# An attention-like recommendation layer on one core: spreading row weights half a pair nearer to their row sums

## What is computed

```python
outer = jnp.einsum('bi,bnj->bnij', candidate_ad, goods).reshape(Bs, Ns, Ks * Ks)
k_b = jnp.broadcast_to(candidate_ad[:, None, :], (Bs, Ns, Ks))
h1 = jnp.concatenate((k_b, goods, outer), axis=-1)
act = jax.nn.sigmoid(h1 @ W1 + b1)          # 36 hidden values
weight = act @ W2 + b2                       # one weight per good
out = jnp.sum(goods * weight, axis=1)        # (2048, 32)
```

## Time and profile before

| | us |
|---|---|
| median of 3 runs | 270.11 |
| lowest and highest | 269.48, 270.95 |
| the profiled execution, device time | 268.84 |
| its span, first to last instruction | 267.0 |
| PE busy | 254.5 (95%) |
| ACT busy | 236.6 (89%) |
| POOL busy | 196.6 (74%) |
| DVE busy | 193.8 (73%) |

### The profile page before, as it was taken

The page is one execution under the profiler, slowest core; times in us unless marked ns, Lnnn a source line. Parts: engine busy times, 40 slices in busy tenths (PEclk is TensorE's granted clock), DMA queues, the critical chain, the costliest instruction groups (busy, mean ns, idle before and its releaser), DMA issues.

```text
span 267.0 us, 18217 instructions
## 1 busy us (share of the span) xinstructions
PE 254.5 (95%) x7492; PEld 150.3 (56%) x7492; DVE 193.8 (73%) x1108; ACT 236.6 (89%) x658; POOL 196.6 (74%) x349
## 2 busy tenths in 40 slices
PE   7998999999999999999999999999999999999971
PEld 2425666565565665656656666556565565665630
DVE  0890277777777877877777778777787777877886
ACT  2897999999999999999999999999999999999840
POOL 1300787887887888788788788878878878887872
PEclk9999999999999999999999999999999999999996
DMA  5880766787777777777777777777777877777200
GB/s 204 253 300 16 230 196 199 242 229 210 241 224 211 237 220 227 230 218 230 211 223 237 211 236 226 212 239 217 219 224 221 234 219 225 225 210 231 65 0 11
DMA packets 38195, 54.84 MB, mean 205 GB/s; under 512 B 4240, under 2 KB 37904, under 8 KB 38032
## 3 DMA queue, kind: packets, MB, share of 16 engines
q1 hardware_dynamic: 37872, 54.15, 67.1%
q10 hardware_dynamic: 288, 0.32, 0.3%
HBM read 54.19 MB, written 0.26 MB: 204 GB/s over the span
## 4 chain that ended last, share of the span: by engine, by line
PE 91%; ACT 2%; DMA 2%; DVE 2%; issue 1%; POOL 1%; POOLq 0%; DVEq 0%
PE z_ps L337 28%; PE w_ps L384 26%; PE x_ps L360 16%; PE s_ps L422 6%; PE x_ps L422 6%; PE z_ps L289 2%; ACT act L495 2%; DMA act<-w_outer 2%; PE s_ps L337 2%; DVE goods L535 2%; PE s_ps L289 1%; PE x_ps L289 1%; PE x_ps L302 1%; PE w_ps L289 0%; POOL top L255 0%
## 5 line engine op out<-in xcount | busy, mean ns | idle before, releaser
L495 ACT ACTIVATE act<-z_ps,bias 128x200 f32<-128x200 f32 x448 | 149.8, 441 | 13.0 <-PE z_ps L337 7.6
L535 DVE CUSTOM_DVE_ANT_0 goods<-s_ps,goods 128x200 f32<-128x200 f32 x248 | 80.5, 362 | 30.9 <-PE w_ps L422 30.9
L337 PE MATMUL z_ps<-goods,wm_ring 32*32 32x200 f32 x3360 | 77.8, 339 | 1.7 <-issue 1.6
L255 POOL TENSOR_SCALAR top<-whole,consts 128x200 bf16<-128x200 f32 x64 | 50.1, 782 | 22.4 <-DVE whole L527 16.3
L337 PEld LDWEIGHTS z_ps<-goods,wm_ring 32*32 32x32 f32 x3360 | 46.1, 103 | 20.6 <-issue 11.9
L535 DVE CUSTOM_DVE_ANT_0 goods<-x_ps,goods 128x200 f32<-128x200 f32 x124 | 40.5, 364 | 22.7 <-PE s_ps L422 22.7
L384 PE MATMUL w_ps<-act,consts 128*32 128x200 f32 x1008 | 55.7, 339 | 0.0
L360 PE MATMUL x_ps<-goods,wx 128*32 128x200 f32 x1024 | 55.3, 333 | 0.0
L259 POOL TENSOR_SCALAR mid<-rest,consts 128x200 bf16<-128x200 f32 x64 | 50.1, 782 | 6.3
L535 DVE DVE_READ_ACCUMULATOR2_ANT out_stage<- 128x1 f32 x512 | 42.6, 83 | 0.0
L482 ACT ACTIVATE wm_ring<-wm 128x256 f32<-128x256 f32 x60 | 42.4, 706 | 0.0
(11 more groups left out here) (53 smaller groups left out, 212.7 us busy)
## 6 DMA issues: line engine op xcount, KB each, us to landing
goods<-goods_t SPq DMA_DIRECT2D x256, 200.0 KB, 2.7
act<-cand_r SPq DMA_DIRECT2D x1, 1024.0 KB, 5.4
act<-cand_u SPq DMA_DIRECT2D x1, 256.0 KB, 2.8
out_t<-out_stage SPq DMA_DIRECT2D x4, 64.0 KB, 2.6
consts<-small ACTq DMA_DIRECT2D x1, 164.5 KB, 5.4
act<-w_outer ACTq DMA_DIRECT2D x1, 144.0 KB, 5.6
pick_sb<-pick SPq DMA_DIRECT2D x1, 128.0 KB, 2.8
```

The source lines that it names most:

```text
L255: nc.gpsimd.tensor_scalar(top[:, :], whole[:, q % 2, :], m1, None, ALU.mult).then_inc(part_step, 1)
L337: last = nc.tensor.matmul(z_bank(slot, r)[32 * c:32 * c + 32, N * s:N * s + N], weights(slot, 32 * r, 4 * s + c), goods[32 * r:32 * r + 32 ...
L495: last = nc.scalar.activation(act[:, p % A_SLOTS, r, N * s:N * s + N], z_bank(p, r)[:, N * s:N * s + N], ACT.Sigmoid, bias=bias[:, r, p, s ...
L535: last = nc.vector.tensor_tensor_reduce(goods[:, q % G_SLOTS, v, :], s_bank(q, f, s)[:, N * i:N * i + N], goods[:, q % G_SLOTS, v, :], 1.0 ...
```

## The change

LAG stays 3, but the two places of an iteration take other halves. Place 0 of iteration p now spreads half f = 1 of pair p - 3, and place 1 half f = 0 of pair p - 2. DVE pools in the same new order. A pair's two halves are thus spread in place 1 of iteration q + 2 and place 0 of q + 3, instead of places 0 and 1 of q + 3. With it:

- Place 1 in the loop waits for stack_made and w_kept, place 0 for actx_done and pooled[1][0]. There is a place 1 in iteration 2 already.
- Behind the loop: spread(64, 0), row_sums(64), spread(64, 1), both places of 65, and place 0 of 66.
- For pair 63, DVE makes top and rest itself, into tiles of their own (top_last, rest_last), right behind keep(63); POOL makes mid and stack.
- The banks of a place stay as they were in the loop; the semaphores pooled are now counted by place, and SP's waits follow.

```diff
-        def s_bank(q, f, s):
-            if q + LAG in (PAIRS, PAIRS + 2):
-                return z_ps[:, 2 * f + s, :]
-            if f == 0:
-                return (x_ps, s_ps[1])[s]
-            if s == 1:
-                return w_ps
-            return s_ps[0] if q + LAG > PAIRS else s_ps[1]
+        def s_bank(p, place, s):
+            if p >= PAIRS and (p, place) != (PAIRS + 1, 0):
+                first = 0 if (p, place) in ((PAIRS, 0), (PAIRS + 1, 1)) else 2
+                return z_ps[:, first + s, :]
+            return ((x_ps, s_ps[1]), (s_ps[1], w_ps))[place][s]
...
-        POOLED_FROM = [[LAG - 1, LAG - 1], [LAG, LAG]]
-        STACK_FROM = LAG - 1
+        POOLED_FROM = LAG - 1
+        STACK_FROM = LAG - 2
...
-                        sp.wait_ge(pooled[f][s], POOLED_FROM[f][s] + p - G_SLOTS + 1)
+                        sp.wait_ge(pooled[1 - f][s], POOLED_FROM + p - G_SLOTS + 1)
...
             for q in range(PAIRS):
+                if q < PAIRS - 1:
...
+                else:
+                    pool.wait_ge(last_step, 2)
+                    pool.wait_ge(stack_made, STACK_FROM + q)
+                    left = rest_last
+                nc.gpsimd.tensor_scalar(mid[:, :], left[:, :], m2, None, ALU.mult).then_inc(part_step, 1)
...
-            def spread(p, slot, f):
-                q = slot - LAG
-                if f == 0:
-                    pe.wait_ge(stack_made, p)
-                    if slot < PAIRS:
-                        pe.wait_ge(actx_done, p)
-                    if 1 <= q and slot < PAIRS:
-                        pe.wait_ge(pooled[1][0], p)
...
-                else:
-                    if slot < PAIRS:
-                        pe.wait_ge(w_kept, p)
...
+            def spread(p, slot, place):
+                q, f = (slot - LAG, 1) if place == 0 else (slot - LAG + 1, 0)
+                if slot < PAIRS:
+                    if place == 0:
+                        pe.wait_ge(actx_done, p)
+                        pe.wait_ge(pooled[1][0], p)
+                    else:
+                        pe.wait_ge(stack_made, p)
+                        pe.wait_ge(w_kept, p)
+                elif place == 1:
+                    pe.wait_ge(stack_made, p)
...
-                if p >= LAG:
+                if p >= LAG - 1:
                     spread(p, p, 1)
...
             spread(PAIRS, PAIRS, 0)
+            row_sums(PAIRS, PAIRS)
             spread(PAIRS, PAIRS, 1)
-            row_sums(PAIRS, PAIRS)
-            for p in range(PAIRS + 1, PAIRS + LAG):
-                spread(p, p, 0)
-                spread(p, p, 1)
+            spread(PAIRS + 1, PAIRS + 1, 0)
+            spread(PAIRS + 1, PAIRS + 1, 1)
+            spread(PAIRS + 2, PAIRS + 2, 0)
...
             for p in range(PAIRS + LAG):
-                q = p - LAG
-                if q >= 0:
-                    pool_units(q, 0)
+                if p >= LAG:
+                    pool_units(p, 0)
                 if 1 <= p <= PAIRS:
                     keep(p - 1)
-                if q >= 0:
-                    pool_units(q, 1)
+                if p == PAIRS:
+                    dve.wait_ge(w_kept, PAIRS)
+                    nc.vector.tensor_scalar(top_last[:, :], whole[:, 1, :], m1, None, ALU.mult).then_inc(last_step, 1)
+                    dve.wait_ge(last_step, 1)
+                    nc.vector.tensor_tensor(rest_last[:, :], whole[:, 1, :], top_last[:, :], ALU.subtract).then_inc(
+                        last_step, 1)
+                if LAG - 1 <= p < PAIRS + LAG - 1:
+                    pool_units(p, 1)
```

More of the change, by code:

```diff
@@ L74, in build @@
         rest = sb("rest", [P, N])
+        rest_last = sb("rest_last", [P, N])
         top = sb("top", [P, N], BF16)
+        top_last = sb("top_last", [P, N], BF16)
         mid = sb("mid", [P, N], BF16)
@@ L160, in build @@
         part_step = sem("part_step")
+        last_step = sem("last_step")
         stack_made = sem("stack_made")
@@ L220, in _ @@
                 for s in range(2):
-                    sp.wait_ge(pooled[f][s], POOLED_FROM[f][s] + PAIRS)
+                    sp.wait_ge(pooled[f][s], POOLED_FROM + PAIRS)
             first = PAIR_U * (PAIRS - STORE)
@@ L253, in _ @@
             for q in range(PAIRS):
[L254 to L260, removed]
+                if q < PAIRS - 1:
+                    pool.wait_ge(w_kept, q + 1)
+                    nc.gpsimd.tensor_scalar(top[:, :], whole[:, q % 2, :], m1, None, ALU.mult).then_inc(part_step, 1)
+                    pool.wait_ge(part_step, 3 * q + 1)
+                    nc.gpsimd.tensor_tensor(rest[:, :], whole[:, q % 2, :], top[:, :], ALU.subtract).then_inc(part_step, 1)
+                    pool.wait_ge(part_step, 3 * q + 2)
+                    left = rest
+                else:
[3 more added lines that the diff above has]
+                nc.gpsimd.tensor_scalar(mid[:, :], left[:, :], m2, None, ALU.mult).then_inc(part_step, 1)
+                pool.wait_ge(part_step, 3 * q + 3 if q < PAIRS - 1 else 3 * q + 1)
                 if q >= 2:
                     pool.wait_ge(s_done, 2 * (q - 1))
-                nc.gpsimd.tensor_tensor(stack[:, q % 2, :], rest[:, :], mid[:, :], ALU.subtract).then_inc(
+                nc.gpsimd.tensor_tensor(stack[:, q % 2, :], left[:, :], mid[:, :], ALU.subtract).then_inc(
                     stack_made, STACK_FROM + 1 if q == 0 else 1)
@@ L369, in row_sums @@
                     pe.wait_ge(actx_done, p)
-                if LAG + 1 <= slot < PAIRS:
+                if LAG <= slot < PAIRS:
                     pe.wait_ge(pooled[1][1], p)
@@ L386, in row_sums @@
                 last.then_inc(w_done, 1)
-            def spread(p, slot, f):
-                q = slot - LAG
-                if f == 0:
-                    pe.wait_ge(stack_made, p)
-                    if slot < PAIRS:
-                        pe.wait_ge(actx_done, p)
-                    if 1 <= q and slot < PAIRS:
-                        pe.wait_ge(pooled[1][0], p)
[L399 to L408, removed]
-                else:
-                    if slot < PAIRS:
-                        pe.wait_ge(w_kept, p)
[L413 to L418, removed]
+            def spread(p, slot, place):
[8 more added lines that the diff above has]
+                elif place == 1:
+                    pe.wait_ge(stack_made, p)
+                if (slot, place) == (PAIRS, 0):
+                    pe.wait_ge(z_read, PAIRS)
+                if (slot, place) == (PAIRS + 1, 0):
+                    pe.wait_ge(actx_done, PAIRS)
+                    pe.wait_ge(pooled[1][0], PAIRS)
+                if (slot, place) == (PAIRS + 1, 1):
+                    pe.wait_ge(pooled[0][1], PAIRS)
+                if (slot, place) == (PAIRS + 2, 0):
+                    pe.wait_ge(pooled[1][1], PAIRS + 1)
                 for i in range(2):
@@ L421, in spread @@
                         rows = slice(64 * s, 64 * s + 64)
-                        last = nc.tensor.matmul(s_bank(q, f, s)[:, N * i:N * i + N], pick_sb[rows, 2 * f + i, :],
+                        last = nc.tensor.matmul(s_bank(slot, place, s)[:, N * i:N * i + N], pick_sb[rows, 2 * f + i, :],
                                                 stack[rows, q % 2, :], start=True, stop=True)
@@ L527, in keep, with pool_units @@
                 nc.vector.tensor_scalar(whole[:, p % 2, :], sums_bank(p)[:, 0:N], b2, None, ALU.add).then_inc(w_kept, 1)
-            def pool_units(q, f):
-                dve.wait_ge(s_done, 2 * q + f + 1)
+            def pool_units(p, place):
+                q, f = (p - LAG, 1) if place == 0 else (p - LAG + 1, 0)
+                dve.wait_ge(s_done, 2 * q + 2 - place)
                 for s in range(2):
@@ L535, in pool_units @@
                         last = nc.vector.tensor_tensor_reduce(
-                            goods[:, q % G_SLOTS, v, :], s_bank(q, f, s)[:, N * i:N * i + N], goods[:, q % G_SLOTS, v, :],
-                            1.0, 0.0, ALU.mult, ALU.add, out_stage[:, u:u + 1])
-                    last.then_inc(pooled[f][s], POOLED_FROM[f][s] + 1 if q == 0 else 1)
+                            goods[:, q % G_SLOTS, v, :], s_bank(p, place, s)[:, N * i:N * i + N],
+                            goods[:, q % G_SLOTS, v, :], 1.0, 0.0, ALU.mult, ALU.add, out_stage[:, u:u + 1])
+                    last.then_inc(pooled[place][s], POOLED_FROM + 1 if q == 0 else 1)
             for p in range(PAIRS + LAG):
-                q = p - LAG
-                if q >= 0:
-                    pool_units(q, 0)
+                if p >= LAG:
+                    pool_units(p, 0)
                 if 1 <= p <= PAIRS:
                     keep(p - 1)
-                if q >= 0:
-                    pool_units(q, 1)
+                if p == PAIRS:
[6 more added lines that the diff above has]
+                    pool_units(p, 1)
 def kernel(r_goods, r_candidate_ad, L0_rec_W1, L0_rec_b1, L0_rec_W2, L0_rec_b2):
```

## The result

The changed kernel takes 271.28 us (median of 20 runs, 270.12 to 273.71) against 270.13 us (median of 20, 268.68 to 271.56): a ratio of 1.0048, with a 95% interval of 1.0029 to 1.0067. It is 1.2 us slower. That is just under the 0.5% that the prediction took as measurable, though the interval lies clear of 1, and it is 0.9 us away from the prediction's sum (+0.24). The profiled execution took 270.12 us with a span of 268.3, 1.3 over the one before.

A forecast was written before the change was run, and what follows sets the result against it. TensorE was taken as the bound, with VectorE at the end. Terms -0.64 + 0.08 + 0.63 + 0.17 = +0.24 us take the median from 270.11 to 270.35 us, range 269.0 to 272.6.

The forecast's parts named there:

- the three cases: Whole kernel: faster by over 0.5% (chance 0.06), same within 0.5% (0.75), or slower by more (0.19).
- Tail: keep(63) to the last multiply: four fewer multiplies but two new VectorE operations, 6.09 to 5.45 us, gain 0.64.
- Start: Iteration 2 gets a place 1, which delays its products by 0.08 us.
- Ordinary iterations: Loop iterations without a jump: lost sequencer run-ahead is hidden by TensorE's array, products still 0.28 behind place 1; no cost.
- Jumps: Where the loop jumps back the sequencer is the bound: nine times 0.07 us, 0.63 lost.
- The slip near 208: Place 1 once near 208 us, where POOL's stack ends after it: waiting for the stack costs 0.17 us.
- SP's queue: A pair's four loads start up to 1 us earlier; nothing gained or lost.
- A: Loop jumps: the sequencer's loss is hidden there as well, net -0.4 us, 269.7; chance 0.25.
- E: Tail: not shortened, the two operations and a late stack give back all but 0.2 us, 270.8; chance 0.03.
- B: Place 1, every iteration: the new sequencer instruction is missed, 2.1 to 3.1 us, 272.4 at the former; chance 0.17.
- C: Place 1: POOL's stack arrives late once in three pairs, 1.0 us on top, 271.35; chance 0.10.
- D: Place 0: going from three waits to two saves 0.03 us an iteration, 1.8 in all, 268.5; chance 0.05.

The follow-up runs named there:

- e1: Kernel before plus a long-met pick_loaded wait ahead of keep's at place 1, moving keep's wait into the sequencer; ratio 1.0105 to the kernel before.
- e5: Changed kernel, waits in its order, with POOL's weight lay-out moved so the stack is early; ratio 1.0074 to the kernel before.
- e6: Changed kernel without its second part: POOL makes all four parts of the last pair; ratio 1.01 to the kernel before, 271.92 us.
- e8: Changed kernel with ten more TensorE instructions ahead of everything; ratio 1.0061 to the kernel before.
- e4: Changed kernel with place 1's two waits swapped and POOL's weight lay-out moved so the stack is early; ratio 0.9969 to the kernel before.
- e7: Kernel before with ten more TensorE instructions (five matmuls on zeros) ahead of everything; ratio 0.9986 to the kernel before.
- e2: Kernel before plus a long-met pick_loaded wait behind keep's at place 1, so keep's stays on the weight load; ratio 1.0066 to the kernel before.
- e11: The kernel of e2 with ten more TensorE instructions ahead of everything; ratio 1.0 to the kernel before.
- e12: Kernel before with one more matmul, two instructions, ahead of everything; ratio 0.9974 to the kernel before.
- e9: Kernel before with only the change's second part: VectorE makes top and rest of the last pair; ratio 1.0038 to the kernel before.
- e3: Changed kernel with place 1's two waits swapped, keep's on the weight load and the stack's in the sequencer; ratio 1.0079 to the kernel before.

## Why the prediction came out as it did

The time lay in the range, and the ratio in the most likely of the three cases (no difference within 0.5%), by 0.02%. That was luck in part: 1.3 us that the prediction had at nothing were offset by 0.7 us of relief behind the jumps that it didn't foresee either; without the relief the ratio would have been some 1.007 (an estimate: 0.7 us more on the 1.2 measured). The value was 0.9 us too low; step by step:

- **Tail**, -0.64 expected, -0.70 measured, the last spread of the kernel before at half the clock, as in the rows that the prediction used. The step that took most care was right, down to the length with the two operations (5.45 against 5.39). They took 0.33 and 0.37 with hand-offs of 0.03 (260.94 to 260.97, 261.30 to 261.33), near 0.36 and 0.05. The figures of the Trainium skill ("VectorE: DVE Perf Modes", the section on the TRN2 errata; 0.17 and 0.37) have the second right and the first too short by half, and the gain of 0.82 estimated from them was too much. The stack of pair 63 was "just covered", as forecast.
- **Start**, +0.08 expected, +0.09 measured.
- **Ordinary iterations**, the step that failed. "TensorE's array hides it: products follow at 0.28 whatever the sequencer did." They follow at 0.30 to 0.31 in 35 of the 36 of the stretch measured, +1.3 us. The one left is the slip near 208: there the stack comes last, keep's wait is met 0.06 earlier than usual before the spread starts, and the products follow at 0.28. I had looked for what the sequencer's lateness does at the products, where there was room, and not at the spread itself: its first weight load starts on time, the next one comes 0.03 late, and all behind it. That the sequencer hadn't fed it yet is my reading of this; the register step fits it, 0.05 behind the first load in every kernel with the loss (the changed one, e1, e5, e6, e8) and 0.05 to 0.06 ahead of it in the others (medians over the ordinary iterations). e1 shows the loss alone, e4 against e5 that it goes away with the order of two waits. The prediction's own sign for it, a period of 3.66, came true.
- **Jumps**, +0.63 expected from 9 x 0.07; measured 0.12 each, the upper end of its bounds, and -0.09 in the iteration behind (0.12 of relief, less the 0.03 of every iteration). The first is the sequencer again. The second wasn't foreseen, and e7 shows that ten instructions ahead of the loop, with no change in it, give the same relief.
- **The slip near 208**, +0.17 expected, 0.03 measured; place 1 wasn't held by the stack otherwise either. **SP's queue**, nothing expected, nothing seen.

Of the rivals, A (jumps at 0.48) is refuted by 0.58 to 0.62 there, and E by the tail. B came nearest. Its term was mis-sized, 28 ns an iteration against 35 to 51, and its place was wrong: the path from keep's copy to the spread did fit into the 0.11, what didn't was the feed behind it. C, the late stack, is refuted by e5, though the profile's releaser names it. D had no part: place 0 with two waits is preceded by the same 0.32, and the sequencer has one instruction there in each iteration of the loop as before (line 398, then 403), so the third wait had cost none. The rule of the Trainium skill ("Perfetto Trace Analysis", Tensor Engine Instruction), that a waiting weight load leaves the sequencer free, was the right one to weigh. The trace agrees with it: before, the register step starts 0.05 us ahead of the weight load that had been waiting. That run-ahead is what was lost, and the open half, whether it is missed, e1 and e2 answered: yes where the wait ends late, no in ordinary iterations where it was met.

What stays open: what the iteration behind a jump depends on (10 instructions ahead mattered, 2 did not, and e1 and e2 differ with the same number), and why the loop's first turn varies by up to 2 us.

## What to carry to other kernels

On TensorE in these kernels, the first of two waits listed rides on the weight load and the second goes to the sequencer. Where the engine has no slack, list first the signal that comes last, so that the sequencer only meets signals long given: 2.4 us of loop here. The other engines were not tried. A releaser in the trace named the wait that the instruction itself carries, which need not be the one that costs. And a change in two parts is worth testing in parts: here each part of the tail is worth nothing or less without the other.

## What the hardware showed that I had not expected

- A sequencer wait of 51 ns on TensorE that ends late costs 28 ns in an ordinary iteration (median 0.278 to 0.306 from place 1 to the products), in the weight load behind the first; the same instruction with its wait met costs nothing there, and 0.03 us at a jump.
- The iteration behind a loop's jump took 3.65, 3.77 or 3.88 us for the same or nearly the same loop. Ten instructions ahead of the loop brought it to 3.65 twice (e7, e11), two did nothing (e12).
- TensorE's granted clock at the last spread. The stretches around it (span of the stretch, busy time of PE, PEld, DVE, ACT, POOL, then the granted clock) in the kernel before, the changed one and the one in which POOL makes all parts:

```profile
262.00:263.00 1.00, 0.85 (x8) 0.42 (x8) 0.76 (x7) 0.00 (x0) 0.01 (x1) 0.50 0.00 0
```
```profile
263.20:264.00 0.80, 0.52 (x8) 0.28 (x8) 0.80 (x7) 0.00 (x0) 0.03 (x1) 1.00 0.00 0
```
```profile
264.30:265.30 1.00, 0.85 (x8) 0.44 (x8) 0.38 (x3) 0.00 (x0) 0.00 (x1) 0.50 0.00 0
```

After 2.93 us without a weight load the eight matmuls ran at 0.50, that is 1.2 GHz, and took 0.85 us; after 2.19 us at the full 2.4 GHz, 0.52. It looks as if the shorter pause kept the clock, but other executions deny it. In e9 the pause was 2.99 us and the clock full, in e3 it was 2.16 us and the clock half:

```profile
263.40:264.20 0.80, 0.52 (x8) 0.31 (x8) 0.80 (x7) 0.00 (x0) 0.00 (x0) 1.00 0.00 0
```
```profile
263.40:264.40 1.00, 0.85 (x8) 0.44 (x8) 1.00 (x7) 0.00 (x0) 0.06 (x1) 0.50 0.00 0
```

So the length of the pause alone doesn't decide the clock, and the change can't be credited with it. In the old order the clock shows in the tail (6.09 to 6.10 us from keep(63) to the last multiply at half, 5.94 in e2 at full); in the changed kernel the spread is hidden under VectorE's multiplies, and the tail takes 5.39 at either.
